# Moving small steps between GpSimd, VectorE and ScalarE in a mixture-of-experts layer with chunked recurrence, and shifting the attention's additions by one unit

## The chip, the cores and the metric

One core of one Trainium2 chip runs the whole program. The metric is device time in microseconds (us), as the median of several runs. TensorE (PE) multiplies matrices, VectorE (DVE), ScalarE (ACT) and GpSimd (POOL) do elementwise work, and SyncE (SP) issues most of the DMAs. Each engine runs its own list of instructions in order. They wait for one another through semaphores.

## The reference

x has 16 sequences of 512 tokens with 128 channels. The layer norm of x feeds two branches, whose product is added to x:

```python
xn = _layernorm(x, axis=-1)
s = _L0_attn_ref(xn, ...)        # RWKV-like recurrence, 16 heads of 8
g = _silu(_L0_ffn_ref(xn, ...))  # shared expert + top 2 of 8 routed experts
x = x + s * g
# the experts
logits = flat @ gate_W.T; probs = softmax(logits); top 2 per token
out_e = (silu(flat @ w1_e) * (flat @ w3_e)) @ w2_e
ffn = 0.5 * shared + 0.5 * sum_e gates * out_e
# the recurrence, in chunks
A = einsum(r, k) * Wmat
y = einsum(A, v) + einsum(r, state) * wb
new_state = ws * state + einsum(k * wk, v)
```

## The kernel before

Everything is in one program, written out by hand with semaphores. Each engine's order is that of its own program function.

**First phase.** The rows of x are normalised and transposed into two f16 parts, a high one and a low one (`xh`, `xl`). A product is formed as high by high, high by low and low by high.

**Expert units.** The expert work is cut into 103 units `v` of 256 tokens: 24 shared units, then 71 routed ones with the last 8 shared units mixed in. A unit has two halves, and `i = 2v + h` numbers the halves. For a half PE does the two up-projections (`pe_up`), ACT the Silu (`act_up`), DVE the gating product `gu` (`dve_up`), ACT its f16 high part `guh` (`act_split`), and then one engine the low part `gul = gu - guh`. That engine is POOL for `i < POOL_LOWS` (`pool_first_low`) and DVE otherwise (`dve_split`). The program has `POOL_LOWS = 12`. `pe_down(v)` needs both low parts, and `dve_up(i)` waits for the low part of half `i - 2`, since `gu` has two buffers. Up to half 24 DVE and ACT also split the next expert's weights, one piece per half (`dve_split_w`, `act_split_w`).

**Sorting by one-hots.** In the halves 13 to 40 (28 slots) the list of sorted tokens is built by 128 small products `pe_hot(n)`, three slots later on PE. Each needs a lane one-hot, `hot_lane` (128x128 f16), and a block one-hot, `hot_block` (128x142 f16). The lane one-hots come in 16 sets of 8: POOL makes 11 sets, one one-hot at a time (`pool_lanes`), and DVE makes 5 sets, each in one 128x1024 instruction (`dve_lane_set`). DVE makes all 128 block one-hots (`dve_blocks`), four or five in a slot.

**Attention.** After the experts come 16 attention units, `u = 0..15`, of four sequences by 128 tokens. All engines run a pipelined loop. DVE applies the decays (`dve_decay`), updates the states (`dve_state`), selects heads (`dve_select`) and forms the result (`dve_gate(u)`). POOL masks the states (`pool_mask`), forms low parts (`pool_low`), and adds the expert rows: `pool_add(u, 0)` adds the two gathered ones and `pool_add(u, 1)` the shared one. It also adds x (`pool_end(u)`). ACT applies Silu to the summed rows (`act_moe(u)`). SP loads and stores. These waits matter here:

```python
def dve_gate(u):      # waits s_out(u), moe_silu(u), and
    V.wait_ge(sem[f"stored{s}"], 16 * (u // 2))       # the store of unit u-2
def sp_moe(u):        # into ring slot u % 3, waits dve_gate(u-3)
def sp_end(u):        # waits pool_end(u)
def act_moe(u):       # waits pool_add(u, 1)
# ACT: ... act_high(2*(u-2)+1); act_moe(u-1); act_kv(u, 0) ...
def pe_kv(u, 1):      # waits the ACT copy act_kv(u, 0), same PSUM bank
```

## Time and profile before

| | |
|---|---|
| median of 3 runs | 791.26 us (791.19 to 791.54) |
| profiled execution, its own time | 789.28 us |
| its span | 787.5 us |
| mean granted TensorE clock | 0.98 |
| PE busy | 671.5 us (85%) |
| DVE busy | 604.0 us (77%) |
| POOL busy | 511.1 us (65%) |
| ACT busy | 454.9 us (58%) |

Busy shares are averages over three phases: up to about 180 us the first phase and the shared units, to about 575 us the routed units, then the attention. A timeline row gives the start, how long the instruction took (or several merged ones, then with x4), and in brackets how long the engine stood idle before it and what ended the idle time. An instruction can start a little before the one ahead of it has fully ended, so a step costs the distance to the next start.

### The profile page before, as it was taken

How to read it: one execution, taken by the hardware profiler on the slowest of the kernel's cores; microseconds unless marked ns; L12 is line 12 of the kernel's file. 1: busy time of each engine (PE TensorE's matmuls, PEld its weight loads, DVE VectorE, ACT ScalarE, POOL GpSimd, SP SyncE). 2: the span in 40 equal slices, each digit the busy share in tenths (PEclk: the TensorE clock that was granted, in tenths of full speed). 3: DMA queues.
4: the chain of work that ended last, by engine and by line, in shares of the span. 5: the costliest groups of instructions: out<-in, count | busy, mean ns of one | idle time of the engine just before them, and what ended most of it. 6: DMA issues, size and time to landing. Idle time of an engine off the chain costs nothing. (4 is left out here: it accounts for less than half of the span.)

```text
span 787.5 us, 26010 instructions
## 1 busy us (share of the span) xinstructions
PE 671.5 (85%) x9696; PEld 569.7 (72%) x9696; DVE 604.0 (77%) x1352; ACT 454.9 (58%) x984; POOL 511.1 (65%) x565
## 2 busy tenths in 40 slices
PE   3677877897999999999999999999969878787772
PEld 2465666786887879999999999999856655555551
DVE  6989998986767787777777776777729878787773
ACT  6766655454666656766766667777635444353430
POOL 2434899625777777777777777777654554554542
PEclk9999999999999999999999999999969999999996
DMA  9922310201211233433333343334373446546442
GB/s 248 251 83 83 119 55 1 15 2 33 50 53 51 73 103 105 146 104 111 108 105 110 103 143 104 107 104 103 99 240 110 144 130 196 168 157 211 125 126 80
DMA packets 106041, 87.83 MB, mean 112 GB/s; under 512 B 20610, under 2 KB 90884, under 8 KB 105924
## 3 DMA queue, kind: packets, MB, share of 16 engines
q1 hardware_dynamic: 96836, 66.96, 28.4%
q0 software_dynamic: 9088, 19.21, 9.4%
q8 instruction: 85, 1.39, 0.8%
q14 instruction: 32, 0.26, 0.1%
HBM read 51.40 MB, written 34.73 MB: 109 GB/s over the span
## 5 line engine op out<-in xcount | busy, mean ns | idle before, releaser
L697 ACT CAST hidden<-hidden 128x512 f16<-128x512 f32 x206 | 127.3, 618 | 185.4 <-DVE hidden L1075 185.4
L1081 DVE TENSOR_TENSOR hidden<-hidden 128x512 f16<-128x512 f32 x194 | 134.0, 691 | 79.9 <-ACT hidden L697 79.5
L569 POOL DMA_INDIRECT srows<-normed_rows,source x142 | 148.1, 1043 | 65.0 <-issue 39.1
L578 POOL DMA_INDIRECT expert_rows<-ybuf,dest x142 | 152.5, 1074 | 46.0 <-issue 41.4
L1075 DVE TENSOR_TENSOR hidden<-hidden,banks 128x512 f32<-128x512 f32 x206 | 140.2, 681 | 33.1 <-ACT hidden L692 32.6
L1377 PE MATMUL banks<-sxh,wwords 128*128 128x256 f16 x568 | 155.1, 273 | 3.7 <-issue 2.6
L1394 PE MATMUL banks<-wwords,hidden 128*128 (+1 forms) x824 | 145.4, 221 | 14.3 <-DVE hidden L1081 10.8
L1378 PE MATMUL banks<-sxl,wwords 128*128 128x256 f16 x568 | 155.0, 273 | 0.0
L1379 PE MATMUL banks<-sxh,wwords 128*128 128x256 f16 x568 | 154.9, 273 | 0.0
L1395 PE MATMUL banks<-wwords,hidden 128*128 (+1 forms) x824 | 144.7, 220 | 0.0
L1396 PE MATMUL banks<-wwords,hidden 128*128 (+1 forms) x824 | 144.6, 220 | 0.0
L692 ACT ACTIVATE hidden<-banks 128x512 f32<-128x512 f32 x206 | 122.2, 593 | 2.9 <-PE banks L1379 2.3
L1394 PEld LDWEIGHTS banks<-wwords,hidden 128*128 128x128 f16 x824 | 81.0, 98 | 20.5 <-DVE hidden L1081 11.5
L1162 DVE TENSOR_TENSOR wwords<-banks,wmat 128x1024 f32<-128x1024 f32 x64 | 76.5, 1216 | 14.8 <-PE banks L1491 14.7
L1377 PE MATMUL banks<-xh,wwords 128*128 128x256 f16 x256 | 70.5, 275 | 17.0 <-DVE hidden L1075 16.7
L1395 PEld LDWEIGHTS banks<-wwords,hidden 128*128 128x128 f16 x824 | 81.0, 98 | 1.5
L1396 PEld LDWEIGHTS banks<-wwords,hidden 128*128 128x128 f16 x824 | 81.1, 98 | 0.0
L557 POOL TENSOR_SCALAR rows<-cst,sxl 128x128 f16<-128x128 f32 x88 | 73.8, 857 | 6.0 <-PE banks L1325 6.0
L764 ACT ACTIVATE wwords<-stage,cst 128x512 f32<-128x512 f32 x64 | 42.7, 716 | 55.7 <-DMA stage<-r_rows 55.7
L1378 PE MATMUL banks<-xl,wwords 128*128 128x256 f16 x256 | 70.4, 275 | 0.0
L1379 PE MATMUL banks<-xh,wwords 128*128 128x256 f16 x256 | 70.3, 275 | 0.0
L1377 PEld LDWEIGHTS banks<-sxh,wwords 128*128 x568 | 55.4, 98 | 14.7 <-issue 8.6
(187 smaller groups left out, 1549.9 us busy)
## 6 DMA issues: line engine op xcount, KB each, us to landing
rows<-x SPq DMA_DIRECT2D x32, 256.0 KB, 3.3
rows<-expert_rows SPq DMA_DIRECT2D x32, 256.0 KB, 4.4
normed_rows<-rows SPq DMA_DIRECT2D x16, 256.0 KB, 3.9
r_rows<-rows SPq DMA_DIRECT2D x32, 128.0 KB
rd_rows<-rows SPq DMA_DIRECT2D x32, 128.0 KB
stage<-r_rows SPq DMA_DIRECT2D x16, 256.0 KB, 4.4
k_rows<-rows SPq DMA_DIRECT2D x32, 128.0 KB
kd_rows<-rows SPq DMA_DIRECT2D x32, 128.0 KB
```

The costliest lines, as they stand in the source:

```text
L569: G.indirect_dma_start(srows[:, r % NXB, t, :], None, rows_in, bass.IndirectOffsetOnAxis(source[:, r * TPU + t:r * TPU + t + 1], 0)).then_ ...
L578: G.indirect_dma_start(rows_out, bass.IndirectOffsetOnAxis(dest[:, r * TPU + t:r * TPU + t + 1], 0), ybuf[:, r % NYB, t, :], None).then_in ...
L692: A.activation(sg[:, i % 2, :], psum[2 * (i % 2)][:, :], ACT.Silu, scale=1.0 / SW).then_inc(sem["silu"], 1)
L697: A.copy(guh[:, v % 2, h * 2 * UNIT:(h + 1) * 2 * UNIT], gu[:, i % 2, :]).then_inc(sem["gu_hi"], 1)
L1075: V.tensor_tensor(gu[:, i % 2, :], sg[:, i % 2, :], psum[2 * (i % 2) + 1][:, :], ALU.mult).then_inc(sem["gated"], 1)
L1081: V.tensor_tensor(gul[:, v % 2, s], gu[:, i % 2, :], guh[:, v % 2, s], ALU.subtract).then_inc(sem["gu_lo"], 1)
L1377: T.matmul(o, a, mh, start=True, stop=False)
L1378: T.matmul(o, a, ml, start=False, stop=False)
L1379: k = T.matmul(o, b, mh, start=False, stop=True)
L1394: T.matmul(o, guh[:, v % 2, s], a, start=(c == 0 and t == 0), stop=False)
L1395: T.matmul(o, guh[:, v % 2, s], b, start=False, stop=False)
L1396: k = T.matmul(o, gul[:, v % 2, s], a, start=False, stop=(c == FC - 1 and t == TPU - 1))
```

## The change

It has three parts. Low parts: `POOL_LOWS` goes from 12 to 44. One-hots: DVE makes 12 of the 16 lane sets and POOL 4, spread over the slots; ACT makes every fourth block one-hot in two instructions, `Abs` into a scratch tile and `Relu` out of it. Attention: POOL's order within its loop and the unit for which it adds are moved, and SP issues in another order.

```diff
-            return m % 3 == 2
+            return m % LANE_SETS != LANE_SETS - 1
+        def by_scalar(n):
+            return n % 4 == 0
...
-        POOL_LOWS = 12
+        POOL_LOWS = 2 * FIRST - 4
...
                 if u + KRING < NA:
+                    sp_kd(u + KRING)
                     sp_k(u + KRING)
-                    sp_kd(u + KRING)
                     sp_rd(u + KRING)
+                if u > 0:
+                    sp_end(u - 1)
+                if u + 1 < NA:
+                    sp_x(u + 1)
                 if u + PRING < NA:
                     sp_moe(u + PRING)
-                if u + 1 < NA:
-                    sp_x(u + 1)
-                if u > 0:
-                    sp_end(u - 1)
...
             for u in range(-2, NA + 3):
+                if at(u - 2):
+                    pool_end(u - 2)
                 if at(u - 1):
                     pool_low(2 * (u - 1))
                     pool_low(2 * (u - 1) + 1)
+                if at(u):
+                    pool_add(u, 1)
                 if at(u + 1):
-                    pool_add(u + 1, 1)
                     pool_mask(2 * (u + 1) + 1)
                 if at(u + 2):
                     pool_mask(2 * (u + 2))
-                    pool_add(u + 2, 0)
-                if at(u - 2):
-                    pool_end(u - 2)
+                if at(u + 1):
+                    pool_add(u + 1, 0)
...
+            def act_apart(n):
+                t, k = hot_of(n)
...
+                A.activation(apart[:, n // 4 % 2, :], count16[:, 0:NBLK], ACT.Abs, scale=-1.0,
+                             bias=block_f[:, t, k:k + 1]).then_inc(sem["hot_apart"], 1)
+            def act_block(n):
...
+                A.activation(hot_block[:, n % NHOT, :], apart[:, n // 4 % 2, :], ACT.Relu,
+                             scale=C("token")[:, 16 + t % 16:16 + t % 16 + 1],
+                             bias=C("token")[:, t % 16:t % 16 + 1]).then_inc(sem["hot_scalar"], 1)
...
+                    mine = [n for n in hots(2 * v + h - HOT_FIRST) if by_scalar(n)]
+                    for n in mine:
+                        act_apart(n)
                     act_split(v, h)
+                    for n in mine:
+                        act_block(n)
...
-                        dve_blocks(n)
+                        if not by_scalar(n):
+                            dve_blocks(n)
```

Line numbers move too, so the same work has two. On DVE the first slots of the one-hots read as follows before; L1075 is `dve_up`, L890 `dve_split_w`, L985 `dve_blocks`, L994 `dve_lane_set` and L1081 `dve_split`.

```order
L1075 TENSOR_TENSOR hidden<-hidden,banks 128x512
L890 SCALAR_TENSOR_TENSOR wwords<-stage,wwords 128x512
L985 TENSOR_SCALAR rows<-sxl,sxh,cst 128x142 x5
L1081 TENSOR_TENSOR hidden<-hidden 128x512
L1075 TENSOR_TENSOR hidden<-hidden,banks 128x512
L890 SCALAR_TENSOR_TENSOR wwords<-stage,wwords 128x512
L985 TENSOR_SCALAR rows<-sxl,sxh,cst 128x142 x4
L1081 TENSOR_TENSOR hidden<-hidden 128x512
```

The same engine now; L1112 is `dve_up`, L927 `dve_split_w`, L1022 `dve_blocks` and L1031 `dve_lane_set`.

```order
L1112 TENSOR_TENSOR hidden<-hidden,banks 128x512
L927 SCALAR_TENSOR_TENSOR wwords<-stage,wwords 128x512
L1022 TENSOR_SCALAR rows<-sxl,sxh,cst 128x142 x3
L1031 TENSOR_TENSOR rows<-cst,sxl 128x1024
L1112 TENSOR_TENSOR hidden<-hidden,banks 128x512
L927 SCALAR_TENSOR_TENSOR wwords<-stage,wwords 128x512
L1022 TENSOR_SCALAR rows<-sxl,sxh,cst 128x142 x3
L1112 TENSOR_TENSOR hidden<-hidden,banks 128x512
```

The low part is gone from DVE, a slot has three or four block one-hots in place of four or five, and six of the twelve slots that also split weights hold a lane set.

On POOL, in the attention, one turn of the loop before is: `pool_mask` twice (L597), `pool_add(.., 0)` (L610), `pool_end` (L621), `pool_low` twice (L604), `pool_add(.., 1)` (L615). The brackets hold the semaphores waited for.

```order
L597 TENSOR_TENSOR rows<-hidden,cst 128x256 [waits inter,state]
L597 TENSOR_TENSOR rows<-stage,cst 128x256 [waits inter,state]
L610 TENSOR_TENSOR rows<-rows 128x512 [waits picked1]
L621 TENSOR_TENSOR rows<-rows 128x512 [waits x_again0,s_read]
L604 TENSOR_TENSOR hidden<-hidden,wwords 128x256 [waits y_hi] x2
L615 TENSOR_TENSOR rows<-rows,ffn 128x512 [waits pair_added]
```

The turn that ends unit 0 in the changed kernel:

```order
L610 TENSOR_TENSOR rows<-hidden,cst 128x256 [waits inter,state]
L610 TENSOR_TENSOR rows<-stage,cst 128x256 [waits inter]
L623 TENSOR_TENSOR rows<-rows 128x512 [waits picked2]
L634 TENSOR_TENSOR rows<-rows 128x512 [waits x_again0,s_read]
L617 TENSOR_TENSOR hidden<-hidden,wwords 128x256 [waits y_hi] x2
L628 TENSOR_TENSOR rows<-rows,ffn 128x512 [waits pair_added]
```

The kinds of instruction follow each other in the same circle as before. What moved is the unit: unit 0 was ended behind the addition for unit 4 (ring slot 1), and is now ended behind that for unit 2 (slot 2), and both additions stand one unit later against the ones around them.

On ACT nothing moved in the attention. These rows of the changed kernel are the same in the kernel before but for their line numbers: `act_inter` (L788), `act_high` twice (L803), `act_moe` (L808), the `act_kv` copy (L782), `act_mask` (L796).

```order
L788 COPY hidden<-banks 128x512 [waits ysel,inter]
L803 CAST wwords<-hidden 128x256 [waits s_out,ysel]
L803 CAST wwords<-hidden 128x256 [waits ysel]
L808 ACTIVATE rows<-rows 128x512 [waits moe]
L782 COPY wwords<-banks 128x512 [waits av,upd,kv]
L796 ACTIVATE wwords<-stage,cst 128x512 [waits local,r_in1] x2
```

The Silu stands between the second high part and the copy. In POOL's program the addition that it waits for used to be one loop turn ahead of that, and is now in the same turn.

## Rows read from the trace of the kernel before

**Rows 1.** The source view of DVE's gating line L1187: idle time before it

```profile
  DMA out<-rows: 28.2, 12
```

**Rows 2.** DVE in the timeline of the attention

```profile
593.42 1.23 DVE L1162 TENSOR_TENSOR wwords<-banks,wmat 128x1024 f32<-128x1024 f32 x1 [0.16 <-PE banks L1491]
...
603.46 1.23 DVE L1162 TENSOR_TENSOR wwords<-banks,wmat 128x1024 f32<-128x1024 f32 x1
...
625.85 1.22 DVE L1162 TENSOR_TENSOR wwords<-banks,wmat 128x1024 f32<-128x1024 f32 x1
...
762.88 1.21 DVE L1162 TENSOR_TENSOR wwords<-banks,wmat 128x1024 f32<-128x1024 f32 x1
```

**Rows 3.** POOL in the timeline of the attention, one turn

```profile
627.54 0.74 POOL L597 TENSOR_TENSOR rows<-hidden,cst 128x256 f32<-128x256 f32 x1 [3.64 <-DVE hidden L1151]
...
631.47 1.29 POOL L610 TENSOR_TENSOR rows<-rows 128x512 f32<-128x512 f32 x1 [2.51 <-DMA rows<-expert_rows]
...
633.95 1.30 POOL L604 TENSOR_TENSOR hidden<-hidden,wwords 128x256 f16<-128x256 f32 x2
```

**Rows 4.** ACT in the timeline of the attention: Silu, then the copy

```profile
619.21 0.63 ACT L776 ACTIVATE rows<-rows 128x512 f32<-128x512 f32 x1
619.74 0.56 ACT L750 COPY wwords<-banks 128x512 f32<-128x512 f32 x1
```

**Rows 5.** PE in the timeline of the attention

```profile
610.23 0.33 PE L1433 MATMUL banks<-cst,wwords 128*128 128x128 f32 x1
...
612.37 1.12 PE L1491 MATMUL banks<-wwords,rows 32*64 32x256 f32 x32
```

**Rows 6.** PE at the start of the attention

```profile
585.27 1.12 PE L1471 MATMUL banks<-wwords,rows 64*64 64x64 f32 x16 [1.33 <-POOL rows L597]
```

**Rows 7.** DVE in the timeline of the one-hot slots

```profile
86.67 0.67 DVE L1075 TENSOR_TENSOR hidden<-hidden,banks 128x512 f32<-128x512 f32 x1
...
103.11 0.68 DVE L890 SCALAR_TENSOR_TENSOR wwords<-stage,wwords 128x512 f16<-128x512 f32 x1
103.72 1.35 DVE L985 TENSOR_SCALAR rows<-sxl,sxh,cst 128x142 f16<-128x142 f16 x5
104.99 0.68 DVE L1081 TENSOR_TENSOR hidden<-hidden 128x512 f16<-128x512 f32 x1
...
124.50 0.67 DVE L1075 TENSOR_TENSOR hidden<-hidden,banks 128x512 f32<-128x512 f32 x1
...
132.33 0.69 DVE L1075 TENSOR_TENSOR hidden<-hidden,banks 128x512 f32<-128x512 f32 x1 [2.52 <-ACT hidden L692]
132.93 1.22 DVE L994 TENSOR_TENSOR rows<-cst,sxl 128x1024 f16<-128x1024 f32 x1
134.07 1.05 DVE L985 TENSOR_SCALAR rows<-sxl,sxh,cst 128x142 f16<-128x142 f16 x4
...
170.62 0.67 DVE L1075 TENSOR_TENSOR hidden<-hidden,banks 128x512 f32<-128x512 f32 x1
```

**Rows 8.** The same timeline just behind the slots

```profile
172.75 0.69 DVE L1075 TENSOR_TENSOR hidden<-hidden,banks 128x512 f32<-128x512 f32 x1
...
174.73 0.68 DVE L1075 TENSOR_TENSOR hidden<-hidden,banks 128x512 f32<-128x512 f32 x1
```

**Rows 9.** ACT's groups by shape: count, busy us, mean ns

```profile
L663 ACT ACTIVATE rows<-rows,ffn 128x128 f32<-128x128 f32 x32 | 14.1, 486 | 0.3 <-DVE ffn L877 0.3
...
L771 ACT CAST wwords<-hidden 128x256 f16<-128x256 f32 x32 | 13.0, 406 | 24.2 <-DVE hidden L1178 24.2
```

**Rows 10.** Source views of L547 and L985: duration ns, minimum/median/maximum

```profile
L547 POOL TENSOR_TENSOR hidden<-hidden x12: 1155/1348/1494, 50.2 to 82.3; 128x512 f16<-128x512 f32 x12
...
L985 DVE TENSOR_SCALAR rows<-sxl,sxh,cst x128: 303/317/442, 87.9 to 169.8; 128x142 f16<-128x142 f16 x128
```

**Rows 11.** DVE and POOL in one stretch of the timeline, ahead of the slots

```profile
79.30 1.65 DVE L890 SCALAR_TENSOR_TENSOR wwords<-stage,wwords 128x512 f16<-128x512 f32 x1
...
79.19 1.22 POOL L547 TENSOR_TENSOR hidden<-hidden 128x512 f16<-128x512 f32 x1 [0.90 <-ACT hidden L697]
```

More of the change, by code:

```diff
@@ L196, in build @@
         signed = take([P, NBLK])
+        apart = base[:, 0, :].bitcast(F16).rearrange("p (a b) -> p a b", a=2)
         early = carve(wwords[:, FREE_EXPERTS * EW // 2:EXPERTS * EW // 2])
@@ L337, in on_vector, with slot_of, pool_lanes_at @@
         def on_vector(m):
-            return m % 3 == 2
-        def lane_sets(i):
-            return [n // LANES for n in hots(i) if n % LANES == 0]
+            return m % LANE_SETS != LANE_SETS - 1
+        def by_scalar(n):
+            return n % 4 == 0
+        def slot_of(n):
+            return next(i for i in range(HOT_SLOTS) if n in hots(i))
+        def pool_lanes_at(i):
+            for m in range(LANE_SETS - 1, NHOTS // LANES, LANE_SETS):
+                first, each = (LANES_KNOWN, 1) if m < LANE_SETS else (HOT_FIRST + HOT_LAG + slot_of(LANES * (m - LANE_SETS + 1) - 1) + 1, 2)
+                at = (i - first) * each
+                if 0 <= at < LANES:
+                    return [m * LANES + at + j for j in range(each)]
+            return []
+        LANES_KNOWN = 12
         ROUTE_CHOSEN = 12
@@ L547, in pool_first_low, with pool_lane @@
                 G.tensor_tensor(gul[:, v % 2, s], gu[:, i % 2, :], guh[:, v % 2, s], ALU.subtract).then_inc(sem["gu_lo_first"], 1)
-            def pool_lanes(m):
-                if m == 0:
+            def pool_lane(n):
+                m = n // LANES
+                if n == LANES * (LANE_SETS - 1):
                     G.wait_ge(sem["lanes"], 1)
                     G.wait_ge(sem["normed_out"], 16 * nb)
-                if m >= LANE_SETS:
+                if m >= LANE_SETS and n % LANES == 0:
                     G.wait_ge(sem["hot_used"], LANES * (m - LANE_SETS + 1))
-                for n in range(LANES):
-                    t, k = hot_of(m * LANES + n)
-                    G.tensor_scalar(hot_lane[:, m % LANE_SETS, n, :], C("count")[:, 0:P], lane_f[:, t, k:k + 1], None,
-                                    ALU.is_equal).then_inc(sem["hot_lane"], 1)
+                t, k = hot_of(n)
+                G.tensor_scalar(hot_lane[:, m % LANE_SETS, n % LANES, :], C("count")[:, 0:P], lane_f[:, t, k:k + 1], None,
+                                ALU.is_equal).then_inc(sem["hot_lane"], 1)
             def pool_sorted(r):
@@ L626, in pool_program @@
                 pool_norm(b)
-            for i in range(2 * SHARED):
+            for i in range(2 * FIRST):
                 if i < POOL_LOWS:
                     pool_first_low(i)
-                for m in lane_sets(i - HOT_FIRST + 1):
-                    if not on_vector(m):
-                        pool_lanes(m)
+                for n in pool_lanes_at(i):
+                    pool_lane(n)
             for r in range(ROUTED + SCATTER_LAG):
@@ L980, in dve_blocks @@
                 t, k = hot_of(n)
-                if n == 0:
+                if n == 1:
                     V.wait_ge(sem["blocks"], 2)
```

18 lines of the change are left out of this document (15 added, 3 removed).

## The prediction

> **What bounds the kernel now.** I read the waits first, then the timelines of the two places that the change touches. The attention is held by a loop of waits, not by an engine. Its 16 turns start with the DVE decay L1162, and I call the start of turn w T(w). T(1) to T(2) took 603.46 - 593.42 = 10.04 us with no wait for a store in it [rows 2]. T(2) to T(15) took 762.88 - 603.46 = 159.42 us, 12.26 a turn. The reader should see the difference in one row: the gating L1187 waited 12 times for the DMA that stores `out`, 28.2 us in all [rows 1]. The loop is: `dve_gate(w)` frees a ring slot, SP then issues the loads of the expert rows for unit w+3, POOL's addition for that unit waits 2.51 us for them [rows 3], `pool_end` stands behind that addition, the store behind `pool_end`, and the next gating behind the store.
>
> In the one-hot slots DVE is the bound. Its rows carry no bracket from one slot to the next. A slot holds gating 0.60 (132.33 to 132.93), weight split 0.61 (103.11 to 103.72), five block one-hots 1.27 (103.72 to 104.99) and the low part [rows 7]. Halves 13 to 24 took 124.50 - 86.67 = 37.83 us, halves 25 to 40 took 170.62 - 124.50 = 46.12 us.
>
> **One-hot slots, step by step.** DVE loses the low part, about 0.60 us to the next start. It loses a quarter of the block one-hots: 128/28 = 4.57 a slot become 3.43, at 1.27/5 = 0.254 each, so 0.87 us a slot. A lane set costs 134.07 - 132.93 = 1.14 us [rows 7], and there are 12 now where there were 5.
>
> ACT gets a chain that it did not have. Without one-hots a half took 174.73 - 172.75 = 1.98 us [rows 8], in which gating, f16 cast and next Silu follow each other. The `Relu` of a block one-hot stands between cast and Silu, so it lengthens this circle. No row shows it. The nearest is L663, 128 wide with scale and bias both from memory, 486 ns [rows 9]. It ends some 0.09 us behind the next start, as other rows of ACT do (0.63 long, 0.53 apart [rows 4]), so 0.40. From below, half of the plain 256-wide cast of 406 ns is 0.20 [rows 9]. I take 0.40, as L663 has the same operands: 1.98 + 1.14 x 0.40 = 2.44 us a slot. The `Abs` lies ahead of the cast, where ACT waits for DVE anyway. With a weight split in the slot that cover is used up, so I take 2.50 there.
>
> The sum for halves 13 to 24: six slots hold a lane set, 0.60 + 0.61 + 1.14 + 0.87 = 3.22 us of DVE. The other six go by ACT, 2.50. Together 34.3, and I add 0.3 for the port (below): 34.6, a gain of 3.2 us. Halves 25 to 40: six slots with a lane set, 0.60 + 1.14 + 0.87 = 2.61, ten by ACT at 2.44, together 40.1. ACT's router exponential stays as a stall of 2.52 [rows 7]. The gate work on DVE and the table loads on ACT now fall on the engine that sets the pace in light slots, for which I add 2.0, chosen between nothing and twice that. That makes 44.6, a gain of 1.5. Both together: **-4.7 us**. With the `Relu` at 0.20 it would be 0.23 less in 16 slots, -8.4.
>
> Low parts on POOL take 1.155 to 1.494 us [rows 10] and not 0.68. They are hidden: a low part starts behind gating (0.67) and cast, ends some 2.6 us after its gating started, and the gating that waits for it comes two halves, over 4 us, later. If slots get shorter than 1.3 us this cover is gone, and nothing here is near that.
>
> **The port.** In the trace a low part on POOL and a two-input instruction on DVE exclude each other. L890 took 0.68 us as a rule but 1.65 when it started at 79.30, inside a low part that ran from 79.19 for 1.22 us: it ended 0.54 after that one [rows 11]. Now POOL runs a low part in 32 more halves. Most start 1.35 us after the gating, when the weight split is over; the lane sets hold POOL back rather than the reverse. The block one-hots took 0.30 to 0.44 us each, though POOL made lane one-hots beside most of them [rows 10], so I let them run free. The Trainium skill, page "SBUF — State Buffer", section "SBUF: two separate sides", says that the shared pair of ports is an exclusive lock, held for the whole instruction, and that VectorE takes it in a two-port mode as well as with two inputs from SBUF; by that, f16 one-input instructions such as these one-hots would be shut out too. The trace agrees for L890. For the one-hots it does not so far, and this is a rival below.
>
> **Attention, step by step.** The store wait goes. Ends now come one turn earlier (the addition ahead of `pool_end` has data that was loaded a turn before), so 28.2 us of waiting are freed and a turn could take the 10.04 that T(1) to T(2) took. What is late next is the sum of the expert rows. `act_moe(w)` waits for `pool_add(w, 1)`, which POOL now reaches in the same turn, behind everything else in it; behind `act_moe` on ACT stands the copy `act_kv`, and PE's `pe_kv(w+1, 1)` waits for that copy, since it writes the same bank. Behind PE's are `pe_out`, `pe_local` and the next decay. So the turn is one chain. From T(w), with the rows of the same kinds:
>
> - 1.69 to the first mask (625.85 to 627.54) [rows 2, 3]
> - two masks, 0.70 each to the next start
> - first addition and end, 2.48 (631.47 to 633.95), so 1.24 each; two low parts 1.25; second addition, of the same shape as the first, 1.28 to its end [rows 3]. POOL: 8.1 us after T(w)
> - 0.06 to wake ACT, Silu 0.53 to the next start, copy 0.56 [rows 4], 0.05 to wake PE
> - PE from `pe_kv` to `pe_local` 612.37 - 610.23 = 2.14, `pe_local` 1.12 [rows 5], 0.11 to wake DVE
>
> That is 12.67 us. The PE piece varies by 0.08, and I take 12.63. The gain of each freed wait is thus given back inside the turn. T(2) to T(15) becomes 13 x 12.63 = 164.2. The first turn has no `pool_end` (1.24 less) but then waits for ACT's high part, so I take 12.0. T(1) to T(15) was 169.46 and becomes 176.2: **+6.8 us**. The turns that never waited pay for most of it.
>
> At the start mask 1 no longer stands behind an addition that waits for its load, and PE's 1.33 us go [rows 6]; some of it is lost in slow work behind, **-0.9**. The tail behind T(15) has no next `pe_kv` and stays. SP's new order costs nothing: each load is needed at least 4 us after it lands by the same turn of 12.6. In the routed units nothing changes.
>
> **Sum.** -4.7 + 6.8 - 0.9 = +1.2 us. The profiled execution took 789.28, so 790.5 for it; the median of the runs is 1.98 above it: **792.5 us**. A measurement of this kernel tells changes from about 0.2% on, 1.6 us; this one is just inside.
>
> **Rivals.**
>
> - *ACT does not wait for the addition, or the wait is hidden.* Place: `act_moe`. For it speaks that the reordering frees 28.2 us of real waits and that DVE is busy for 10.04 of a turn. Against it, POOL's work alone puts the addition 8.1 us behind T(w), and no other work of ACT stands ahead of its Silu long enough to cover that in a turn of 10.04. Then all 14 turns take 10.04, 140.6 instead of 169.46, and the time is 791.3 - 4.7 - 28.9 - 0.9 = 757 us. It decides the sign as soon as a turn takes less than 12.4 us. Chance 0.13.
> - *The one-hots on ACT are cheap and the turn ends a little below my chain.* `Relu` at 0.20 and 12.45 a turn: 791.3 - 8.4 + 4.3 - 0.9 = 786 us. Chance 0.15.
> - *The port shuts out the block one-hots.* In a slot with a weight split they would start at 1.2, wait for the low part's end at about 2.55, and end near 3.15; all 12 early slots lose some 0.6. The slots gain nothing: 792.5 + 7 = 799.5 us. Behind the split's last half they run ahead of the low part, which limits the loss. Chance 0.12.
> - *As summed above,* 789 to 796 us. Chance 0.60.
>
> **How the numbers follow.** The range 784 to 801 us leaves out the first rival (0.13) and a few hundredths of the ends. Faster by over 0.2%: 0.13 + 0.15 + 0.03 of the main case = 0.31. Within: 0.27 of the main case and 0.02 of the rivals' edges = 0.29. Slower: the rest of the main case, 0.30, and the port, 0.10, = 0.40.
>
> **What would show it.** Right: no idle time before the gating by a store, but ACT's Silu waiting for POOL's second addition and PE's `pe_kv` for the ACT copy, in each turn; turns of 12.6 us; slots at 2.4 to 2.6 without and 2.6 to 3.3 with a lane set; ACT one-hots of 0.4 us; no new idle time of PE by low parts. Wrong: turns near 10 us, block one-hots over 1 us long, or the Silu early. A prediction that rests on two opposite terms of 5 and 6 us is wrong in sign if either is off by a third.

## The result

The changed kernel took 812.44 us, the median of 4 runs (812.2 to 812.82), and the kernel before, run on the same chip, 791.23 us (785.22 to 791.54). The ratio is 1.0287, with a 95% interval of 1.0238 to 1.0336. The forecast was 792.5 us with a range of 784 to 801, so the time lies above the range. "Slower" had the largest of the three chances, 0.40, but the sum itself said +1.2 us, which is no change, and +21.2 us came.

### The profile after

The first lines of the page of the changed kernel, busy time by engine, and further down the TensorE clock in 40 slices (of 20.3 us each):

```profile
span 810.4 us, 26026 instructions
...
PE 684.6 (84%) x9696; PEld 580.5 (72%) x9696; DVE 602.0 (74%) x1295; ACT 477.7 (59%) x1048; POOL 500.5 (62%) x541
...
PEclk9999999999999999999999999999899999989896
```

PE makes the same 9696 matmuls and yet is busy 13 us longer than before. That is the first sign: the same work at a lower clock. Two windows of the attention, the kernel before and then the changed one (columns: stretch and its length, busy us and count for PE, PEld, DVE, ACT and POOL, granted clock, DMA share, GB/s):

```profile
600.00:700.00 100.00, 79.96 (x1992) 57.68 (x1984) 81.03 (x125) 45.26 (x84) 51.37 (x56) 1.00 0.53 159
```

```profile
600.00:700.00 100.00, 76.53 (x1761) 56.43 (x1745) 74.23 (x114) 40.88 (x75) 47.36 (x53) 0.93 0.50 149
```

Every engine does less in 100 us, and the clock is at 0.93 where it was at 1.00. The waits of the changed kernel between 600 and 790 us (total us, times, longest):

```profile
DVE rows L1224 <- PE banks L1568: 41.2, 14, 3.5
...
PE banks L1474 <- ACT wwords L782: 34.4, 14, 2.5
ACT rows L808 <- POOL rows L628: 33.1, 14, 2.4
```

The wait for a store [rows 1] is gone. In its place ACT's Silu waits for POOL's second addition in every turn, and PE waits for the ACT copy behind that Silu. The start of each turn is the decay, which is now L1199. These rows stand against [rows 2]:

```profile
595.84 1.23 DVE L1199 TENSOR_TENSOR wwords<-banks,wmat 128x1024 f32<-128x1024 f32 x1 [0.36 <-PE banks L1532]
...
608.00 1.23 DVE L1199 TENSOR_TENSOR wwords<-banks,wmat 128x1024 f32<-128x1024 f32 x1 [0.43 <-PE banks L1532]
621.93 1.22 DVE L1199 TENSOR_TENSOR wwords<-banks,wmat 128x1024 f32<-128x1024 f32 x1 [0.43 <-PE banks L1532]
634.46 1.22 DVE L1199 TENSOR_TENSOR wwords<-banks,wmat 128x1024 f32<-128x1024 f32 x1 [0.43 <-PE banks L1532]
648.58 1.23 DVE L1199 TENSOR_TENSOR wwords<-banks,wmat 128x1024 f32<-128x1024 f32 x1 [0.58 <-PE banks L1532]
...
785.82 1.23 DVE L1199 TENSOR_TENSOR wwords<-banks,wmat 128x1024 f32<-128x1024 f32 x1 [0.43 <-PE banks L1532]
```

T(1) to T(15) is 785.82 - 595.84 = 189.98 us, where it was 169.46. The first turn takes 12.16. Of the 13 that follow, three take 12.53, as 634.46 - 621.93, and ten take 13.9 to 14.1, as 648.58 - 634.46 = 14.12. One of the ten, link by link (POOL, ACT, then PE), in the timeline of the changed kernel:

```profile
636.15 0.74 POOL L610 TENSOR_TENSOR rows<-hidden,cst 128x256 f32<-128x256 f32 x1 [6.16 <-DVE hidden L1188]
...
637.54 1.27 POOL L623 TENSOR_TENSOR rows<-rows 128x512 f32<-128x512 f32 x1
...
641.27 1.26 POOL L628 TENSOR_TENSOR rows<-rows,ffn 128x512 f32<-128x512 f32 x1
...
642.56 0.63 ACT L808 ACTIVATE rows<-rows 128x512 f32<-128x512 f32 x1 [2.39 <-POOL rows L628]
643.10 0.57 ACT L782 COPY wwords<-banks 128x512 f32<-128x512 f32 x1
...
643.72 0.33 PE L1474 MATMUL banks<-cst,wwords 128*128 128x128 f32 x1 [2.48 <-ACT wwords L782]
```

From T(w) to PE's restart are 643.72 - 634.46 = 9.26 us; the forecast's links up to there add up to 9.30. The rest runs at another speed: 648.58 - 643.72 = 4.86 us in this turn. In the turn ahead of it PE's restart was at 631.18, so that piece took 634.46 - 631.18 = 3.28. The windows of PE alone (busy us and count, granted clock, DMA share, GB/s) show why. First the piece behind the restart in the good turn, then the idle stretch and the piece in the long one:

```profile
631.20:633.30 2.10, 2.10 (x40) 1.00 0.03 8
640.90:643.40 2.50, 0.33 (x16) 1.00 0.80 229
...
644.20:647.60 3.40, 3.40 (x37) 0.51 0.02 5
```

For 3.4 us the granted clock is at 1.2 GHz, and it falls just as PE comes back from 2.5 us with nothing to do. Before, PE's idle time in a turn came in two pieces, 1.1 to 1.4 us behind the gating and 0.7 to 1.7 before `pe_out`, with several us of matmuls between them, and the clock stayed at 2.4 GHz.

**The slots.** Halves 13, 25 and 41 start here in the changed kernel (before: [rows 7]):

```profile
86.57 0.69 DVE L1112 TENSOR_TENSOR hidden<-hidden,banks 128x512 f32<-128x512 f32 x1 [0.58 <-ACT hidden L706]
...
128.43 0.67 DVE L1112 TENSOR_TENSOR hidden<-hidden,banks 128x512 f32<-128x512 f32 x1
...
176.60 0.69 DVE L1112 TENSOR_TENSOR hidden<-hidden,banks 128x512 f32<-128x512 f32 x1 [0.65 <-ACT hidden L706]
```

So 13 to 24 took 41.86 us (37.83 before, 34.6 forecast) and 25 to 40 took 48.17 (46.12 before, 44.6 forecast). DVE and POOL in an early slot, and three free block one-hots in a late one:

```profile
102.84 1.76 DVE L1022 TENSOR_SCALAR rows<-sxl,sxh,cst 128x142 f16<-128x142 f16 x3
103.05 1.15 POOL L560 TENSOR_TENSOR hidden<-hidden 128x512 f16<-128x512 f32 x1 [2.51 <-ACT hidden L711]
...
140.45 0.77 DVE L1022 TENSOR_SCALAR rows<-sxl,sxh,cst 128x142 f16<-128x142 f16 x3
```

Three block one-hots take 1.76 us beside a low half on POOL and 0.77 without it. Over all 96 of them (minimum/median/maximum in ns) one went up to 1253 where [rows 10] had 442 at most:

```profile
L1022 DVE TENSOR_SCALAR rows<-sxl,sxh,cst x96: 306/317/1253, 88.9 to 175.6; 128x142 f16<-128x142 f16 x96
```

**Where the 22.9 us of span went.** 189.98 - 169.46 = 20.5 us in the 14 turns of the attention and 595.84 - 593.42 = 2.4 us ahead of T(1). The slots lost 6.1 us, and T(0) came at 586.49 instead of 581.15, 5.3 us late. T(0) to T(1) then took 9.35 us where it had taken 12.27, so over half of that was taken up again before T(1). Behind T(15) nothing changed.

### The profile page after: what moved, and what is told of

Its sections match the earlier page's. It is cut to its first block and busy times, and to the rows that moved or that the text cites. A ratio compares the mean times of both kernels' runs of the same rounds, so it can differ in the third digit from the quotient of the medians.

```text
span 810.4 us, 26026 instructions
## 1 busy us (share of the span) xinstructions
PE 684.6 (84%) x9696; PEld 580.5 (72%) x9696; DVE 602.0 (74%) x1295; ACT 477.7 (59%) x1048; POOL 500.5 (62%) x541
## 5 line engine op out<-in xcount | busy, mean ns | idle before, releaser
L591 POOL DMA_INDIRECT expert_rows<-ybuf,dest x142 | 152.5, 1074 | 46.1 <-issue 41.4
L1112 DVE TENSOR_TENSOR hidden<-hidden,banks 128x512 f32<-128x512 f32 x206 | 140.4, 681 | 42.6 <-ACT hidden L706 42.2
L1118 DVE TENSOR_TENSOR hidden<-hidden 128x512 f16<-128x512 f32 x162 | 112.2, 693 | 77.7 <-ACT hidden L711 77.4
L560 POOL TENSOR_TENSOR hidden<-hidden 128x512 f16<-128x512 f32 x44 | 57.9, 1316 | 60.6 <-ACT hidden L711 60.5
L1199 DVE TENSOR_TENSOR wwords<-banks,wmat 128x1024 f32<-128x1024 f32 x64 | 76.6, 1218 | 19.3 <-PE banks L1532 19.3
L610 POOL TENSOR_TENSOR rows<-hidden,cst 128x256 f32<-128x256 f32 x16 | 11.8, 736 | 113.3 <-DVE hidden L1188 113.3
```

What stands on the lines that cost most here:

```text
L591: G.indirect_dma_start(rows_out, bass.IndirectOffsetOnAxis(dest[:, r * TPU + t:r * TPU + t + 1], 0), ybuf[:, r % NYB, t, :], None).then_in ...
L1112: V.tensor_tensor(gu[:, i % 2, :], sg[:, i % 2, :], psum[2 * (i % 2) + 1][:, :], ALU.mult).then_inc(sem["gated"], 1)
L1118: V.tensor_tensor(gul[:, v % 2, s], gu[:, i % 2, :], guh[:, v % 2, s], ALU.subtract).then_inc(sem["gu_lo"], 1)
```

## The experiments

The theory after the result (T) had two mechanisms. In the attention the late second addition makes a chain of 12.53 us a turn, and PE's one long idle stretch in it brings the clock down, 1.5 us in most turns. In the slots POOL's low half shuts out DVE's block one-hots. The rivals are stated with each run.

### The attention alone, and the slots alone

The kernel before with only the change to `pool_program`'s attention loop and to SP's order, as in the diff above:

> The kernel before with only the attention changed: POOL's new order in a turn and SP's new order of loads and stores; the one-hot slots stay as in before. Theory T: the whole loss of the change sits here, in two terms. The chain through the late second addition lasts 12.53 us a turn (the changed kernel has three such turns), and in most turns TensorE's granted clock falls to 1.2 GHz for a stretch of 3.4 us, which makes the turn 13.9 to 14.1. Then T(1) to T(15) takes about 190 us instead of 169.46 and the time is about 791.2 + 20.5 - 0.9 = 811. Rival P (the prediction's own sum): turns of 12.6, time about 791.2 + 6.8 - 0.9 = 797. Rival S: the longer turns are an effect of what the changed slots leave behind; then turns are near 12.3 and the time stays near 791.

Measured: 808.45 us, ratio 1.0253 (1.0230 to 1.0277). T(1) to T(15) was 781.37 - 590.81 = 190.56 us, with four turns at 12.54 and the others at 13.8 to 14.2. Theory T holds, P and S don't. T(1) came 2.6 us earlier than before; in the five kernels here that have the slots of before and POOL's `pool_end` moved ahead, and were traced on a chip as fast as this one, T(1) lies between 589.73 and 591.92.

The changed slots with the attention of before:

> The changed kernel's one-hot slots (low halves on GpSimd, lane sets on VectorE, a quarter of the block one-hots on ScalarE) with the attention of before. Theory T: the slots cost what the span up to T(1) shows, 2 to 5 us more than before: 793 to 796. Rival P (the prediction's sum for the slots): 4.7 us less, 786.5. Rival N: no difference, since the attention's waits for transfers take up what is late at its start: 791.

Measured: 792.89 us, ratio 1.0066 (1.0040 to 1.0093). T(0) came at 586.27, 5.1 us late, and T(1) at 595.36, 1.9 us late. Theory T holds for the place and the sign; P is wrong.

### GpSimd's order or SyncE's

Only `pool_program` changed, SP's order as before:

```diff
             for u in range(-2, NA + 3):
+                if at(u - 2):
+                    pool_end(u - 2)
...
+                if at(u):
+                    pool_add(u, 1)
```

> The kernel before with GpSimd's new order in a turn of the attention, and SP's old order of loads and stores. Theory T: GpSimd's order alone makes the chain of 12.53 and the clock's falls; SP's order costs and gives nothing: turns as with both, time about 808 to 811 where before is 789 to 791 (ratio 1.025). Rival O: SP's old order, with the store last, brings the store wait back in front of the gating: turns over 14, time above 812. Rival S: it was SP's order that cost, turns stay near 12.3, 790.

Measured: 807.15 us, ratio 1.0226 (1.0184 to 1.0269), T(1) to T(15) 779.67 - 589.73 = 189.94 us, the first turn 12.15, three at 12.53 or 12.54, ten at 13.9 to 14.1, and no wait for a store. POOL's order alone makes the whole loss, as the forecast had it, and SP's order neither adds nor saves.

### Is it the clock?

The changed attention with the slots of before, and in each turn 24 matmuls whose result nobody reads, ahead of `pe_kv(u, 1)`:

```diff
+                if 2 <= u < NA:
+                    T.wait_ge(sem["state"], 2 * u)
+                    for n in range(24):
+                        T.matmul(psum[1][:, 0:P], f2y[:, :], f2y[:, :], start=True, stop=True)
                 if at(u):
                     pe_kv(u, 1)
```

> As the kernel with only the attention changed, with 24 added 128x128 matmuls in each turn on TensorE, into a piece of PSUM that is rewritten afterwards, placed where TensorE waits 2.5 us for ScalarE's copy. Theory T (the falling clock makes ten of thirteen turns 1.4 us longer, and it falls since TensorE's idle time now comes in one piece): with the wait filled the granted clock stays at 2.4 GHz, turns take 12.5 to 12.7 us, and the time is about 14 us below the kernel with only the attention changed, near 797. Rival W (the turns are longer for some other reason, such as waits on a transfer, and the clock only shows alongside): the clock stays up and the turns stay at 13.9, time near 811. Rival D: the added matmuls outlast the wait; then turns are longer than 13.9 and PE's wait for the copy is gone.

Measured: 793.99 us, ratio 1.0066 (1.0041 to 1.0091), 14.5 us less than without the added work. Two starts of turns, T(2) and T(15), and three windows of PE, over the added matmuls, the wait behind them, and the piece behind the restart:

```profile
604.08 1.23 DVE L1164 TENSOR_TENSOR wwords<-banks,wmat 128x1024 f32<-128x1024 f32 x1 [0.43 <-PE banks L1493]
...
767.16 1.23 DVE L1164 TENSOR_TENSOR wwords<-banks,wmat 128x1024 f32<-128x1024 f32 x1 [0.43 <-PE banks L1493]
```

```profile
661.00:662.50 1.50, 1.50 (x32) 1.00 0.57 158
662.50:663.50 1.00, 0.05 (x1) 1.00 0.81 227
663.50:666.90 3.40, 3.37 (x80) 1.00 0.03 8
```

The 13 turns take 163.08 us together, 12.54 each, and the clock stays at 2.4 GHz. From PE's restart to the next decay it is 3.28 us again, as in the changed kernel's good turns. T(1) to T(15) is 767.16 - 591.92 = 175.24 us, within a microsecond of the 176.2 that the forecast had for the changed kernel. So the forecast's chain was right to 0.1 us a turn, and the clock is all that it lacked in the attention. Work that nobody needs made the program 14.5 us faster than the same kernel without it, on the same chip.

Then two smaller fills, to see whether the length of the unbroken pause counts or the amount of work. Eight of the same matmuls, once at the start of the wait (waiting for `state` as above), once in its middle, which is this edit to the kernel with 24:

```diff
-                    T.wait_ge(sem["state"], 2 * u)
-                    for n in range(24):
+                    T.wait_ge(sem["moe"], u)
+                    for n in range(8):
```

> As the kernel with only the attention changed, with 8 added 128x128 matmuls in each turn (0.44 us) placed at the start of TensorE's wait for ScalarE's copy: the idle stretch is 2.05 us instead of 2.5, in one piece. Theory G (the length of the unbroken idle stretch brings the clock down): the clock still falls in most turns, which stay at 13.9, time near 808. Theory S (TensorE's share of work in a turn does): same time as the kernel with 8 in the middle, whatever it is. With the clock kept turns are 12.54 and the time is 794.

> The same 8 matmuls, but placed where GpSimd's second addition ends, so that they cut TensorE's wait of 2.5 us into pieces of 1.3 and 0.7 us. Theory G: the clock stays at 2.4 GHz, turns of 12.54, time near 794. Theory S: the same as with the 8 at the start of the wait; if 0.44 us more of work is too little, both stay at 13.9 a turn and 808.

The chip of these two runs took 929.6 us for the kernel before (the last section says where), so I go by the turns, whose lengths are those of the other chips. At the start: T(1) to T(15) 191.1 us, three turns at 12.53 or 12.54. In the middle: 189.5 us, four such turns. Ratios 1.0188 (1.0128 to 1.0248) and 1.0121 (1.0062 to 1.0181). Neither keeps the clock. One turn with the eight in the middle (PE alone; pause, added work, pause, restart):

```profile
779.00:780.30 1.30, 0.02 (x3) 1.00 0.90 236
780.30:780.90 0.60, 0.54 (x8) 1.00 0.85 246
780.90:781.40 0.50, 0.08 (x2) 1.00 0.07 22
781.50:784.80 3.30, 3.30 (x29) 0.50 0.01 2
```

Behind pauses of 1.3 and 0.5 us the clock fell here, and before the change, with two pauses of up to 1.4 and 1.7 us some us apart, it did not. So theory G, by which the longest pause decides, is wrong. Theory S isn't right as it stands either: with the eight in the middle PE's two pauses make 1.9 us in a turn and the clock falls, and before they made 2.5 on average and it stayed. What exactly brings the clock down stays open. What is shown is that in the changed kernel and in the four with its attention and at most eight added matmuls it fell behind idle time gathered near one place, and that filling 1.5 of the 2.5 us there stopped it.

### The additions one unit ahead

Against the attention of the changed kernel:

```diff
-                if at(u):
-                    pool_add(u, 1)
+                if u >= 0 and at(u + 1):
+                    pool_add(u + 1, 0)
+                    pool_add(u + 1, 1)
                 if at(u + 1):
                     pool_mask(2 * (u + 1) + 1)
                 if at(u + 2):
                     pool_mask(2 * (u + 2))
-                if at(u + 1):
-                    pool_add(u + 1, 0)
+                if u == -1:
+                    pool_add(0, 0)
+                    pool_add(0, 1)
```

> The kernel before with the new order on SP and with POOL's end ahead of both additions, but with both additions for the unit one ahead (in the changed kernel the second addition is for the unit that ScalarE wants in this same turn). Theory T: the store wait is gone as in the changed kernel, and ScalarE's Silu no longer waits for the addition, so a turn is bound by DVE's own work, 10.0 to 10.2 us, with TensorE busy enough to keep its clock; T(1) to T(15) near 142 instead of 169.46, time near 791.2 - 28.9 + 1 = 761 to 764. Rival L: the additions wait for loads of the expert rows again, since they are needed a turn earlier, and the turns stay at 12.3, time 791. Rival C: the shorter turns are given back by the lower clock, turns near 11.5, time near 780.

Measured: 761.76 us, ratio 0.9656 (0.9632 to 0.9680). That is 27.1 us less than the kernel before and 46.7 less than the kernel with only the attention changed, on the same chip. The starts of the turns, T(1), T(2) and T(15):

```profile
591.15 1.23 DVE L1166 TENSOR_TENSOR wwords<-banks,wmat 128x1024 f32<-128x1024 f32 x1 [0.35 <-PE banks L1495]
...
601.19 1.22 DVE L1166 TENSOR_TENSOR wwords<-banks,wmat 128x1024 f32<-128x1024 f32 x1
...
735.80 1.22 DVE L1166 TENSOR_TENSOR wwords<-banks,wmat 128x1024 f32<-128x1024 f32 x1
```

There is no bracket at 601.19: DVE comes straight from its other work, and the turn that ends there, like most, takes 10.04 us, what T(1) to T(2) took before. T(1) to T(15) is 144.65 us. The clock stays up in these turns, and one turn of 12.28 us holds a pause of PE of 1.64 us that ended in "issue", which means that no wait in the profile explains it. Theory T holds.

### The port, seen in the slots

The next kernels all have the additions one ahead. First the changed slots with them:

> The changed kernel with both additions of the attention one unit ahead, so the changed one-hot slots and the short turn together. Theory T: the two parts add up. The one-hot slots cost 2 to 5 us as in the kernel with only the shared units changed, the attention saves about 27: 762 + 2 to 5, so 764 to 767. Rival: the attention's start hides the slots' loss, 762. Half 13 to 25 near 41.9 us, 25 to 41 near 48.2, as in the changed kernel.

Measured: 762.81 us, ratio 0.9684 (0.9644 to 0.9724); halves 13 to 24 took 41.86 us, 25 to 40 took 48.14. The slots' loss is there in full, but the time is only 1 us above the 761.76 of the kernel without it, which ran on another chip. My 764 to 767 was missed. The traces show why: T(1) came at 594.74 instead of 591.15, so 3.6 us of the loss reached the attention, and T(1) to T(15) took 141.69 us instead of 144.65, as the other kernel's trace has more of the long single turns. Against a second measurement of that kernel, the 760.51 us further down, the loss is 2.3 us.

Then POOL's low half is made a plain copy. This leaves out the low parts, and it is a probe and no version to use. The edit applies to all 44 halves, those ahead of the slots too:

```diff
-                G.tensor_tensor(gul[:, v % 2, s], gu[:, i % 2, :], guh[:, v % 2, s], ALU.subtract).then_inc(sem["gu_lo_first"], 1)
+                G.tensor_copy(gul[:, v % 2, s], gu[:, i % 2, :]).then_inc(sem["gu_lo_first"], 1)
```

> As the kernel with the changed one-hot slots and the additions one ahead, but GpSimd's low half in the shared units is a plain copy of the gated f32 values to f16 instead of their difference to the high half: one input instead of two. It leaves out the low parts of the hidden activations there. Two readings of why three block one-hots beside a low half take 1.76 us instead of 0.77: U, only GpSimd's two-input instruction holds the port pair that VectorE's f16 one-input instructions use; then the three take 0.77 to 0.8 beside the copy as well, halves 13 to 25 shrink from 41.9 to about 37 and 25 to 41 from 48.2 to about 43, and the time is 8 to 12 us below that kernel. V, any GpSimd instruction of this kind holds it; then they still take about 1.7 and the time moves only by what the copy is shorter than the difference (under 3 us).

Measured: 751.28 us, ratio 0.9536 (0.9498 to 0.9574), 11.5 us below the one before it. Halves 13 to 24 took 35.67 us, 25 to 40 took 45.10, so 9.2 us less in the slots, and half 13 began 3.4 us earlier. By the time alone theory U would have won. The rows of this kernel say otherwise:

```profile
62.49 0.62 POOL L560 CAST hidden<-hidden 128x512 f16<-128x512 f32 x1 [1.85 <-ACT hidden L713]
...
99.57 0.61 POOL L560 CAST hidden<-hidden 128x512 f16<-128x512 f32 x1 [1.35 <-ACT hidden L713]
99.61 1.21 DVE L1024 TENSOR_SCALAR rows<-sxl,sxh,cst 128x142 f16<-128x142 f16 x3
```

Three one-hots take 1.21 us beside the copy and not 0.77, so the copy shuts them out as well, only for a shorter time. Both theories had a number wrong: V in that the copy had to cost as much as the difference. The first row is a copy beside which DVE did nothing; it is as long as the one beside the one-hots, so POOL is not slowed by them.

> As the kernel with the changed one-hot slots and the additions one ahead, but from half 12 on the low halves are back on VectorE; lane sets (most on VectorE) and the quarter on ScalarE stay. Theory T (GpSimd's low half shuts out the block one-hots): VectorE pays 0.6 us for a low part in each of 28 halves and gets back 0.7 to 1.0 us in each with block one-hots beside it, so halves 13 to 41 are between 4 us longer and 6 us shorter than 90.0, time 758 to 770. Rival N (no exclusion, low halves on GpSimd are a pure relief): 28 x 0.6 = 17 us longer, 780.

The edit is `POOL_LOWS = 12`. Measured: 760.71 us, ratio 0.9659 (0.9620 to 0.9698). Halves 13 to 24 took 38.12 us and 25 to 40 took 47.80, together 85.92 where the low halves on POOL gave 90.00. To relieve DVE of 28 low parts of 0.60 us, 16.8 us of work, cost 4.1 us in the slots (2.1 in the time). Theory T holds and N falls.

### The port by itself

Behind the last unit of the kernel with the additions one ahead, DVE makes block one-hots alone and then beside three kinds of POOL instructions. DVE's instruction, and POOL's in the phase with the difference:

```diff
+                V.tensor_scalar(xl[:, 142 * n:142 * n + 142], xh[:, 0:142], pick[:, 0:1], zsum[:, 0:1], ALU.is_equal, ALU.mult).then_inc(sem["probe_w"], 1)
...
+                G.tensor_tensor(xl[:, 2048 + 512 * n:2560 + 512 * n], r32[:, 0, :], yh[:, 0, :], ALU.subtract).then_inc(sem["probe_p"], 1)
```

> The kernel with the additions one ahead, and behind its last unit a probe: VectorE runs twelve block one-hots of 142 wide (f16 in and out, both scalars from memory) alone, then beside GpSimd's two-input 128x512 difference (three of them), its plain copy f32 to f16 of 128x512 (six), its lane one-hot of 128 wide (six); then twelve with f32 in and out alone, beside the difference, and beside the copy; all of it twice. Only the probe's rows are of interest; it adds 60 to 90 us of span. Alone twelve should take 12 x 0.24 = 2.9 us. Theory V: every GpSimd difference and copy of 512 wide holds the port pair for its whole length against VectorE's f16 one-input instructions, so twelve take 2.9 + 3 x 1.1 = 6.2 beside the differences and 2.9 + 6 x 0.6 = 6.5 beside the copies; beside lane one-hots 2.9 (as in the slots) or up to 6.5 if these hold it too. Theory U (only two inputs hold it): 2.9 beside copies. The f32 one-hots: if it is VectorE's fast form for f16 that needs the pair, they stay as long as alone beside either; if it is any VectorE instruction, they grow in the same way.

The probe ran once, on the chip where the kernel before takes 929.6 us; POOL's copies are as long in it as in the row above. The timeline of its first pass; each phase begins with one one-hot of its own (left out) and then has eleven:

```profile
890.42 2.59 DVE L1322 TENSOR_SCALAR xl<-xh,pick,zsum 128x142 f16<-128x142 f16 x11
...
893.27 5.25 DVE L1328 TENSOR_SCALAR xl<-xh,pick,zsum 128x142 f16<-128x142 f16 x11
893.50 3.37 POOL L658 TENSOR_TENSOR xl<-stage,wwords 128x512 f16<-128x512 f32 x3 [3.36 <-DVE xl L1326]
...
898.85 4.59 DVE L1335 TENSOR_SCALAR xl<-xh,pick,zsum 128x142 f16<-128x142 f16 x11
899.09 3.40 POOL L662 CAST xl<-stage 128x512 f16<-128x512 f32 x6 [2.21 <-DVE xl L1333]
...
903.77 3.10 DVE L1342 TENSOR_SCALAR xl<-xh,pick,zsum 128x142 f16<-128x142 f16 x11
904.05 3.59 POOL L666 TENSOR_SCALAR xl<-cst,zsum 128x128 f16<-128x128 f32 x6 [1.56 <-DVE xl L1340]
```

Alone eleven take 2.59 us, 0.235 each. Beside three differences they take 5.25, so each difference costs DVE 2.66 / 3 = 0.89 us. Beside six copies it is 2.00 / 6 = 0.33 us each, and beside six lane one-hots 0.51 / 6 = 0.085 us each. With f32 operands, eleven take 2.99 alone, 5.55 beside the differences and 4.76 beside the copies, nearly the same additions, so it isn't the f16 form. The second pass repeated the first within 0.01 us. The durations of the eleven, minimum/median/maximum in ns, beside the differences and beside the copies:

```profile
L1328 DVE TENSOR_SCALAR xl<-xh,pick,zsum x11: 306/309/1209, 893.3 to 898.2; 128x142 f16<-128x142 f16 x11
L1335 DVE TENSOR_SCALAR xl<-xh,pick,zsum x11: 306/634/671, 898.9 to 903.1; 128x142 f16<-128x142 f16 x11
```

Single one-hots are long, and the rest take what they take alone. The numbers fit one one-hot for each difference or copy: 0.89 + 0.235 is 1.12, the spacing of the differences (3.37 / 3), and 0.33 + 0.235 is 0.57, that of the copies (3.40 / 6). That spacing is POOL's own. With f32 one-hots, which take 0.27 us each, it stays at 3.37 and 3.40, and the copy's 0.61 us is its length beside an idle DVE too. So POOL goes at its own pace, and DVE is let through once in each of POOL's instructions. What DVE loses is the spacing less one one-hot. My expectation for the copies, 6 x 0.6, left that one-hot out. Beside the lane one-hots this count does not hold: they are 0.6 us apart and cost 0.085, so DVE does about two one-hots in each.

The Trainium skill, page "SBUF — State Buffer", section "SBUF: two separate sides", says that a VectorE instruction in a two-port mode or with two inputs from SBUF and one of GpSimd lock each other out for the whole instruction. The probe agrees for the difference and the copy, in that no second one-hot gets in during either. For the lane one-hot the cost is 0.085 us of a recorded 0.6, so the recorded length of a GpSimd instruction is no measure of what it costs VectorE.

### ScalarE's quarter, and the best version

The one-hots of ScalarE without the other two edits of the slots:

> The kernel before with the additions one ahead and only one part of the slots' change: ScalarE makes a quarter of the block one-hots; low halves and lane sets stay where they were. Theory T: VectorE is the bound in the slots and loses 32 block one-hots of 0.254 us, 8.1 us in all, and each slot's floor by ScalarE (2.4 to 2.5) lies below VectorE's 2.8 to 3.2; halves 13 to 41 take 84.0 - 8.1 = 76 to 78 us, time 762 - 6 to 8 = 754 to 756, below both kernels. Rival A: the Relu between ScalarE's cast and its next Silu sets the pace, little is gained: 760 to 762.

Measured: 757.6 us, ratio 0.9618 (0.9578 to 0.9657). Halves 13 to 24 took 34.7 us and 25 to 40 took 46.7, 81.4 together, where I had written 76 to 78: the early slots gain 3.1 us, the late ones lose 0.6. In the late slots ACT's circle sets the pace: DVE's gating waited 9 times for ACT between 125 and 170 us, 6.1 us in all, where it had waited once, for 2.5, in the kernel without the quarter. The timeline of ACT in the changed kernel shows the `Relu` (L760) between the cast and the next Silu:

```profile
153.18 0.62 ACT L711 CAST hidden<-hidden 128x512 f16<-128x512 f32 x1 [0.45 <-DVE hidden L1112]
153.71 0.50 ACT L760 ACTIVATE rows<-ybuf,cst 128x142 f16<-128x142 f16 x1
154.11 0.57 ACT L706 ACTIVATE hidden<-banks 128x512 f32<-128x512 f32 x1
```

The `Relu` costs 154.11 - 153.71 = 0.40 us, as forecast. So the quarter was limited to the first 60 one-hots (PE's wait counts follow it):

```diff
-            return n % 4 == 0
+            return n % 4 == 0 and n < SCALAR_BLOCKS
+        SCALAR_BLOCKS = 60
```

> As the kernel with the additions one ahead and a quarter of the block one-hots on ScalarE, but ScalarE takes its quarter only among the first 60 one-hots, those of halves 13 to 25, where VectorE also splits weights; after that VectorE makes all. Theory T: halves 13 to 25 took 34.7 us with the quarter and 37.8 without, 25 to 41 took 46.7 with it and 46.1 without, since there ScalarE's circle of 2.3 to 2.5 us a half is the bound and the Relu stands in it; so this kernel has 34.7 and 46.1 and is 0.6 us faster than the one with the quarter throughout, 757. Rival: the difference of 0.6 is taken up by what comes behind the slots, 757.6 and no difference to be seen.

Measured: 899.42 us, ratio 0.9649 (0.9604 to 0.9695), on the chip where before took 929.6 us, so the time says nothing beside the others. The halves took 34.68 and 46.24 us, as theory T has it. Then all three on one chip:

> The kernel with the additions one ahead again, as the base for the next two on the same chip: about 762 us, 0.966 of before.

> The same with a quarter of the block one-hots on ScalarE throughout. Theory T: halves 13 to 41 take 81.4 us instead of 83.9, so 2.5 us less by the slots, 759.5; the 4.2 us that two chips showed hold 1.7 of difference between chips. Rival: the whole 4.2 is there, 757.6.

> The same with ScalarE's quarter in the early halves alone. Theory T: halves 13 to 25 34.7 us, 25 to 41 46.2, together 80.9, so 0.5 us less than with the quarter throughout. Rival: no difference, or the later stage loses 0.5, since VectorE makes more.

Measured: 760.51 us (ratio 0.9628, 0.9595 to 0.9662), 757.92 (0.9594, 0.9561 to 0.9628) and 756.63 (0.9587, 0.9553 to 0.9621). The halves 13 to 40 took 83.99, 81.38 and 80.89 us. The quarter gives 2.6 us in the time and 2.6 in the slots, as theory T said; the intervals of the ratios overlap, but every run with the quarter was below every run without it. The gain of 1.3 by the early limit agrees in sign with 0.5 in the slots, but here the single runs overlap too, so it is not shown. The last is the best version found: 4.1% faster than before, and by the medians of two chips 6.9% below the changed kernel's 812.44.

## Why the forecast was wrong

**The wait moves from the store to the addition.** Right. No store wait is left; In the turn shown Silu waits 2.39 us for the second addition and PE 2.48 for the copy, and in the 14 turns it is 33.1 and 34.4 us together.

**The turn of 12.63 us.** The chain was right, and 12.53 to 12.54 was measured in the changed kernel's three good turns and in the 13 turns behind T(2) with the fill. The first turn took 12.16, forecast 12.0. What failed is the last link, "PE from `pe_kv` to `pe_local` 612.37 - 610.23 = 2.14, `pe_local` 1.12 [rows 5]", taken from a turn in which PE's clock was up and used for a turn in which PE first stands idle for 2.5 us. It took 4.86 us with the handover instead of 3.28 in ten turns of thirteen. From T(2) to T(15) these are 177.82 - 13 x 12.53 = 14.9 us. The term of +6.8 became +20.5: 14.9 by the clock, less 1.3 by a chain 0.1 us shorter, and 0.2 in the first turn. The forecast named no rival for it, though the chain itself gathered PE's two pauses into one.

**The slots, -4.7 us.** They came out at +6.1. The step that failed is "The block one-hots took 0.30 to 0.44 us each, though POOL made lane one-hots beside most of them [rows 10], so I let them run free". The observation was right, and it was made on the wrong instruction: a lane one-hot costs DVE 0.085 us, a low half 0.89. By the forecast's own sum, as an estimate: the six early slots with a lane set get 3.22 + 0.89 = 4.11 us (4.04 measured on average), and the six without, which the forecast let go by ACT at 2.50, get 0.60 + 0.61 + 0.87 + 0.89 = 2.97 (2.94 measured). So the 0.3 us for the port in the early slots had to be about 8.2, which gives 42.5 for the 41.86 measured.

Step by step in those halves: 37.83 before, 34.68 with the quarter alone, 38.12 with the lane sets as well, 41.86 with the low halves on POOL too. The last step takes 12 x 0.60 = 7.2 us of work away and adds 3.7, so its price is 10.9, and 12 x 0.89 is 10.7: with its low parts back DVE bounds every early slot (0.60 + 0.60 + 0.61 + 0.87 = 2.68 us without a lane set), so the last step shows the whole price. With the copy, at 0.33, the same sum gives 36.3 for the early halves, and 35.67 was measured, so the rest of it was sound there. The late halves took 48.17 against 44.6 forecast. There the forecast had 2.0 us of slow work of its own choosing, and how the 3.6 us divide between that and the port was not taken apart; with the copy 45.10 was measured.

The rival "the port shuts out the block one-hots" was true. Its 0.6 us in each of the 12 early slots is what came over the forecast's sum, 41.86 - 34.6 = 7.3; what it put at nothing is the 3.6 us of the late ones. It had been given 0.12.

**The start, -0.9.** It was -2.6 where only the attention was changed, so this term was mis-sized too. In the changed kernel it took up part of what the slots had lost, which is why only 2.4 us of 6.1 are left at T(1); the slots alone left 1.9.

**SP's order costs nothing.** Right. POOL's order alone gave the same turns.

**ACT's price.** Right, 0.40 us for the `Relu`. That it makes ACT the bound in the light slots was in the sum, and with the quarter alone the late slots took 46.7 us against 46.1 without it: there is nothing to gain there.

**The rival of 757 us** named the right price for an addition that is not waited for: with both additions one ahead and the slots of before, 791.3 - 28.9 - 0.9 = 761.5 by its terms, and 761.76 and 760.51 were measured, where the kernel before took 788.88 and 789.47.

## What to carry to other kernels

When an edit moves a wait, look at what the engines' pauses look like afterwards, and for TensorE price the work behind a gathered pause at the lower of its two clocks; here this term was twice the size of the one that was costed. Before small work goes from VectorE to GpSimd, find what each kind of GpSimd instruction holds up, with that kind and no other: here a relief of 0.60 us cost 0.89. An addition that another engine needs in the same turn belongs one turn ahead, if its data is there: between two kernels that differ only in where the additions stand, on one chip, it made 46.7 us of difference, 808.45 to 761.76. Against the kernel before, whose additions were early enough but held up the store, the gain is 27.

## What the runs showed of the hardware

GpSimd's instructions and VectorE's small ones on the port pair: in the probe a GpSimd difference of 128x512 cost VectorE 0.89 us, a copy of the same size 0.33 and a 128x128 one-hot 0.085, each recorded as 1.15, 0.61 and 0.60 us long. Beside the difference and the copy one VectorE instruction of 0.235 us ran in each, with f32 operands one of 0.27 us, and GpSimd kept its own spacing of 1.12 and 0.57 us.

One of the chips ran the kernel before in 929.6 us where others need 788 to 791. Two rows of the page of the kernel with the early quarter from that chip (group, busy us, mean ns, idle before and its cause):

```profile
L1414 PE MATMUL banks<-sxh,wwords 128*128 128x256 f16 x568 | 162.7, 286 | 29.5 <-issue 22.6
L1416 PE MATMUL banks<-sxh,wwords 128*128 128x256 f16 x568 | 162.4, 286 | 14.5 <-issue 14.2
```

On another chip, in the kernel with the additions one ahead, the first of these groups had 3.9 us of idle time before it, 2.7 of it ended by "issue", and a mean of 273 ns. On the slow chip PE had pauses that no semaphore explains, in the routed units above all, and its granted clock between 300 and 500 us was 0.92 to 0.96 in three kernels traced on it. The attention and the slots were as fast as elsewhere. What made the pauses no row shows.
